# Mixer output normalized into its PSUM bank and added to the residual by VectorE for three batches, in place of GpSimd's sum of two SBUF buffers

## The reference

```python
x = x + layernorm(mixer(layernorm(x)))
x = x + layernorm(ffn(layernorm(x)))

def mixer(h):                       # Wi, Wf, Wg, Wo: 512 x 512
    i, f, g = h @ Wi.T, h @ Wf.T, h @ Wg.T
    gate = sigmoid(f)
    v = silu(i) * (1 - gate)
    o = scan over tokens of  s = gate * s + v
    o = rms_norm(o) * gnorm_w * silu(g)
    return o @ Wo.T
def ffn(h):                         # W1, W3: 2048 x 512, W2: 512 x 2048
    return fwht(silu(h @ W1.T) * (h @ W3.T)) @ W2.T
```

## Time and profile before

| what | value |
|---|---|
| median of 3 runs | 689.96 us |
| the profiled execution's own time | 689.71 us |
| its span, first to last instruction | 687.9 us |
| PE busy | 656.9 us, 95% |
| VectorE busy | 409.8 us, 60% |
| ScalarE busy | 352.8 us, 51% |
| GpSimd busy | 234.1 us, 34% |
| mean granted TensorE clock | 0.995 |

### The profile page before, as it was taken

The page is one execution under the profiler, slowest core; times in us unless marked ns, Lnnn a source line. Parts: engine busy times, 40 slices in busy tenths (PEclk is TensorE's granted clock), DMA queues, the critical chain, the costliest instruction groups (busy, mean ns, idle before and its releaser), DMA issues.

```text
span 687.9 us, 11542 instructions
## 1 busy us (share of the span) xinstructions
PE 656.9 (95%) x4339; PEld 427.8 (62%) x4340; DVE 409.8 (60%) x791; ACT 352.8 (51%) x629; POOL 234.1 (34%) x216
## 2 busy tenths in 40 slices
PE   3898999999999999999979999999999999999995
PEld 2444444444466677677757677777777777777672
DVE  5989898999999999884557113152222215322134
ACT  4999876473675756554525333353333334333332
POOL 1337366665751344164315111221121113121112
PEclk9999999999999999999999999999999999999999
DMA  8992543107344495993984332496223435435002
GB/s 318 406 404 103 129 117 62 61 7 179 122 160 132 169 280 146 329 300 113 266 274 174 111 108 108 136 299 224 108 108 126 170 134 192 146 120 200 3 1 91
DMA packets 60743, 114.12 MB, mean 166 GB/s; under 512 B 40464, under 2 KB 40720, under 8 KB 56080
## 3 DMA queue, kind: packets, MB, share of 16 engines
q1 hardware_dynamic: 60688, 113.39, 49.9%
HBM read 80.87 MB, written 23.07 MB: 151 GB/s over the span
## 4 chain that ended last, share of the span: by engine, by line
PE 64%; DVE 16%; ACT 7%; issue 5%; DVEq 3%; DMA 2%; POOL 2%; SPq 0%; POOLq 0%; ACTq 0%
PE ps L635 21%; PE ps L636 21%; PE ps L637 21%; DVEq L1052 3%; DVE st L1051 2%; ACT junk L914 1%; DVE o_s L1142 1%; ACT ring L835 1%; DMA out<-res 1%; DVE w2t L1306 1%; DVE w2t L1311 1%; DVE mv L1053 1%; ACT junk L921 1%; POOL w2t L1406 1%; DVE ring L1251 1%
## 5 line engine op out<-in xcount | busy, mean ns | idle before, releaser
L635 PE MATMUL ps<-xb,ring 128*128 128x256 f16 (+1 forms) x704 | 212.6, 302 | 3.5 <-DVE ring L1094 1.6
L637 PE MATMUL ps<-xb,ring 128*128 128x256 f16 (+1 forms) x704 | 212.6, 302 | 0.0
L636 PE MATMUL ps<-xb,ring 128*128 128x256 f16 (+1 forms) x704 | 212.6, 302 | 0.0
L1421 POOL TENSOR_TENSOR ring<-sga,ring 128x512 f16<-128x512 f32 x64 | 78.5, 1232 | 316.9 <-ACT ring L1007 316.9
L635 PE MATMUL ps<-ring 128*128 128x256 f16 x384 | 105.2, 274 | 4.4 <-DVE ring L1281 4.3
L636 PE MATMUL ps<-ring 128*128 128x256 f16 x384 | 105.0, 274 | 0.0
L637 PE MATMUL ps<-ring 128*128 128x256 f16 x384 | 105.0, 273 | 0.0
L635 PE MATMUL ps<-w2t,ring 128*128 128x512 f16 x256 | 97.0, 379 | 3.2 <-POOL ring L1421 3.2
L637 PE MATMUL ps<-w2t,ring 128*128 128x512 f16 x256 | 97.0, 379 | 0.0
L636 PE MATMUL ps<-w2t,ring 128*128 128x512 f16 x256 | 97.0, 379 | 0.0
L635 PEld LDWEIGHTS ps<-xb,ring 128*128 128x128 f16 x704 | 69.1, 98 | 40.8 <-issue 3.7
(11 more groups left out here) (165 smaller groups left out, 1033.4 us busy)
## 6 DMA issues: line engine op xcount, KB each, us to landing
ring<-w_comb SPq DMA_DIRECT2D x24, 1792.0 KB, 7.4
ring<-W13t SPq DMA_DIRECT2D x14, 1024.0 KB, 10.6
w_comb<-ring SPq DMA_DIRECT2D x8, 1792.0 KB, 7.0
rows<-L_attn_hidden_states SPq DMA_DIRECT2D x16, 256.0 KB, 5.3
w2t<-W2t SPq DMA_DIRECT2D x8, 512.0 KB, 13.6
res<-L_attn_hidden_states SPq DMA_DIRECT2D x16, 256.0 KB, 4.9
x_rows<-res SPq DMA_DIRECT2D x16, 256.0 KB, 3.4
x1r<-x_rows SPq DMA_DIRECT2D x16, 256.0 KB, 3.6
```

The costliest lines, as they stand in the source:

```text
L635: pe.matmul(dst, a_hi, b_hi, start=start, stop=False, skip_group_check=onto)
L636: pe.matmul(dst, a_hi, b_lo, start=False, stop=False, skip_group_check=onto)
L637: return pe.matmul(dst, a_lo, b_hi, start=False, stop=stop, skip_group_check=onto)
L1421: pool.tensor_tensor(hid(b, c, 1), sga[:, c % 2], hid(b, c, 0), ALU.subtract).then_inc(hid_lo, 1)
```

## The change

ScalarE writes the normed Y back into Y's own PSUM bank for mixer batches 0, 1 and 2, and VectorE adds that bank to `res[:, t]`, in a new step YA. The twelve GpSimd sums YN.0.t to YN.2.t go; batch 3 keeps the old way. The bank is now free only when VectorE's sum is done (`x1_rdy`). ScalarE's wait for the previous batch's sum (which protected the SBUF slot) goes, and GpSimd's YN.3.t gets a wait for the sums before it.

All five lists are written anew around this. Apart from YA and YN each engine runs the same steps as before, in another order; the banks are dealt anew too.

```diff
@@ wait_for_bank
             elif k == "Y":
-                engine.wait_ge(y_norm, TC * n + u + 1)
+                engine.wait_ge(x1_rdy if n < B - 1 else y_norm, TC * n + u + 1)
@@ ScalarE
             def yn(b, t):
                 act.wait_ge(y_ab, TC * b + t + 1)
-                if b > 0:
-                    act.wait_ge(x1_rdy, TC * (b - 1) + t + 1)
-                act.activation(y_rows(t), bank("Y", b, t)[:], ACT.Identity, bias=ab[:, 0, t:t + 1],
+                to = bank("Y", b, t)[:] if b < B - 1 else y_rows(t)
+                act.activation(to, bank("Y", b, t)[:], ACT.Identity, bias=ab[:, 0, t:t + 1],
                                scale=ysc[:, t:t + 1]).then_inc(y_norm, 1)
@@ VectorE
+            def add_residual(b, t):
+                dve.wait_ge(y_norm, TC * b + t + 1)
+                dve.wait_ge(ld_res[t], 16 * (b + 1))
+                dve.tensor_tensor(res[:, t], bank("Y", b, t)[:], res[:, t], ALU.add).then_inc(x1_rdy, 1)
@@ GpSimd
             def yn(b, t):
                 pool.wait_ge(y_norm, TC * b + t + 1)
+                pool.wait_ge(x1_rdy, TC * b + t)
                 pool.wait_ge(ld_res[t], 16 * (b + 1))
```

The parts of the lists that the prediction speaks of, old line first:

```diff
@@ PE_ORDER, start
-XT.0.3:3 AN.0.0:4 AN.1.0:5 GC.0.0:6 F.0.0:7 F.0.1:0 AN.2.0:1 AN.3.0:2 XT.1.0:3 XT.1.1:4
+XT.0.3:3 AN.0.0:4 AN.1.0:5 GC.0.0:6 AN.2.0:7 F.0.0:0 F.0.1:1 AN.3.0:2 XT.1.0:4 XT.1.1:3
@@ PE_ORDER, FFN batch 1, behind the last D of batch 0
-D.0.60 D.0.61 D.0.62 D.0.63 GQ.1.2 GU.1.1 GP.1.3 GR.1.2 GQ.1.3 GU.1.2 D.1.0 GP.1.4 D.1.1 D.1.2 GR.1.3
-D.1.3 D.1.4 D.1.5 D.1.6 GQ.1.4 D.1.7 GP.1.5 GU.1.3 GR.1.4 GU.1.4 GQ.1.5
+D.0.60 D.0.61 D.0.62 GP.1.3 D.0.63 GR.1.2 D.1.0 GU.1.2 GP.1.4 D.1.1 GQ.1.3 GQ.1.4 GR.1.3 GR.1.4 D.1.2
+GP.1.5 D.1.3 GU.1.3 D.1.4 D.1.5 GU.1.4 D.1.6 D.1.7 GP.1.6 GQ.1.5
@@ PE_ORDER, end
-GQ.3.14 GP.3.15 GR.3.14 GQ.3.15 D.3.48 GU.3.14 GR.3.15 D.3.52 GU.3.15 D.3.56 D.3.60 D.3.49
+D.3.36 D.3.37 GR.3.15 D.3.38 D.3.39 GU.3.15 D.3.40 ... D.3.47 D.3.48 D.3.52 D.3.56 D.3.60 D.3.49
@@ ACT_ORDER, ScalarE
-WN.2.0 AT.3.3 WQ.0.0 XT.1.2 ... G.0.2 S.0.1 P.0.1 I.0.3 WN.4.0 XT.1.3 G.0.3
+WQ.0.0 AT.3.2 XT.1.2 AT.3.3 ... G.0.2 F.0.3 S.0.1 P.0.1 WN.4.0 I.0.3 G.0.3 XT.1.3
@@ DVE_ORDER, FFN batch 1
-GU.1.1 UP.1.0 V.0.0 V.0.1 V.0.2 UP.1.1 V.0.3 GR.1.2 W.0.0 W.0.1 GU.1.2 GR.1.3 GU.1.3 W.0.2 W.0.3
-UP.1.2 Z1.3.0 Z1.3.1 Z2.3.0 Z2.3.1 Z1.3.2 UP.1.3 GR.1.4 Z1.3.3 GU.1.4
+GU.1.1 UP.1.0 UP.1.1 V.0.0 V.0.1 W.0.0 V.0.2 GR.1.2 GU.1.2 W.0.1 V.0.3 W.0.2 W.0.3 GR.1.3 GU.1.3
+UP.1.2 GR.1.4 GU.1.4 Z1.3.0 Z1.3.1 Z2.3.0 Z1.3.2 UP.1.3 Z2.3.1 Z2.3.2 Z1.3.3
@@ POOL_ORDER, GpSimd
-FW.0.5 X1.2.0 P.0.0 FW.0.6 FW.0.7
+FW.0.5 FW.0.6 P.0.0 FW.0.7 X1.2.0
@@ SP_ORDER
-NL.0.0 NL.1.0 NL.2.0 UL.0.0 NL.3.0 NL.4.0 UL.1.0 RL.0.0 ...
+UL.0.0 UL.1.0 UL.2.0 UL.3.0 NL.0.0 NL.1.0 UL.4.0 NL.2.0 UL.5.0 NL.3.0 UL.6.0 NL.4.0 UL.7.0 RL.0.0 ...
-WL.1.2 WL.1.3 O.0.0 LR.0.2 LR.0.3 O.0.1 LZ.3.0
+WL.1.2 ZD.2.4 ZD.2.5 ZD.2.6 WL.1.3 LR.0.2 O.0.0 LR.0.3 O.0.1 LZ.3.0
```

255 lines of the change are left out of this document (127 added, 128 removed).

## The result

The changed kernel is slower: 695.62 us (median of 4 runs, 694.72 to 697.37) against 689.74 for the kernel before on the same chip, a ratio of 1.0086 [1.0063, 1.0109], or 5.9 us more where I forecast 6.1 less. The four runs of the kernel before that this rests on (688.73 to 690.3) are on its quick side: beside the experiments it had medians of 691.0 to 692.5 us, and against those the changed kernel would be 3.1 to 4.6 us slower. The sign is sure, the 5.9 may be up to 3 us too much. The profiled execution took 697.37 us, 7.66 more than that of before; it is the slowest of the four runs, so what follows is read from a difference larger than that of the medians.

What follows compares the result with a forecast made beforehand. PE, busy 656.9 of 687.9 us, was taken as the bound, leaving its 31.0 us of standing still: 689.7 - 3.2 - 4.9 - 0.5 + 1.5 + 1.0 = 683.6, with 0.25 for the median 683.9 us; range 679.5 to 689.0.

Steps and rivals of the forecast that it cites:

- FFN batch 1: PE's stall at GU.1.4 and its slow clock, 5.65 us, go by doing VectorE's two sums before the norm: -4.9 us.
- the small stall: In FFN batch 1, a small PE stall in the passage up to GP.1.5: 0.7 us given back from 5.65.
- the stall moves: Rival: x1r as late as before, W.0.2 holds GR.1.3, PE waits at GP.1.5 with slow clock: 688.2 us, chance 0.17.
- The load: VectorE's twelve new sums between 77 and 190 us, 8.3 us less idle time and relief: +1.5 us charged.
- Y's bank, freed one VectorE operation later: PE steps behind YA, such as I.1.1, have another step before them, so the later release costs 0.
- The relief: Removing GpSimd's twelve sums stops them slowing VectorE: 3 us taken, between 0 and 11.4.
- The rival that VectorE starves PE: VectorE's 8.3 us paid in full from batch 1 on, two stalls with half clock: 692.5 us, chance 0.13.
- The start: Reordered first steps and W2's units loaded first: -0.5 us in all, bounds -1.5 and +1.5.
- The 1.2 us wait: At the start, PE's wait for GpSimd's butterfly L1406 ends but mostly moves to F.1.0, behind ScalarE's XT.1.3.
- the tail: End of PE's list: ten D steps, 6.5 us, cover the 3.23 us wait at D.3.56: -3.2 us.
- the tighter product order: PE's GU directly behind GR, and GP close behind GR, more often: 0.1 us for each of nine, +1.0 us.
- my two signs for being wrong: New PE waits over 3 us together between 190 and 330 us, or one of 3 us or more at GP.1.5 or GU.1.3.

Runs made afterwards that it cites:

- e2: Changed kernel's new lists with the old sum of two SBUF buffers put back on GpSimd: 692.91 us, ratio 1.0010 to the kernel before.
- e5: Changed kernel with VectorE's UP.1.3 moved ahead of Z1.3.0: 695.08 us, ratio 1.0048 to the kernel before.
- e4: Kernel before with GR.1.4, GU.1.4 and UP.1.3 ahead of Z1.3.0 in VectorE's list alone: 694.96 us, ratio 1.0033.
- e12: Kernel before with VectorE's new sum for batch 0 alone, GpSimd keeping the other sums: 694.87 us, ratio 1.0048.
- e7: Kernel before plus twelve VectorE operations that nobody waits for and that hold no bank, GpSimd's sums kept: 703.45 us, ratio 1.0166.
- e1: Kernel before, its lists kept, with VectorE's new sum in place of GpSimd's for batches 0 to 2: 700.20 us, ratio 1.0113.
- e10: Changed kernel with UP.1.3 ahead of Z1.3.0 on VectorE and GpSimd, and ScalarE's XT.1.3 ahead of WN.4.0: 695.71 us, ratio 1.0054 to the kernel before.
- e14: e10 and e6 together, with VectorE's XT.1.3 moved earlier and six more FFN batch 1 steps ahead of ZT.3 steps: 694.55 us, ratio 1.0039 to the kernel before.
- e3: Kernel before with six D steps moved behind GU.3.15 in PE's list alone: 686.51 us, ratio 0.9924.
- e15: e14 with the residual sum on GpSimd as in the kernel before: 693.45 us, ratio 1.0017 to the kernel before.
- e16: Kernel before with GpSimd's sums of batches 0 to 2 cut from 512 columns to 1, nothing in their place: 690.71 us, ratio 0.9977.
- e11: e7 with GpSimd's sums of batches 0 to 2 cut from 512 columns to 1: 699.32 us, ratio 1.0101 to the kernel before.
- e18: Changed kernel with the next batch's norm spread in three engines' lists through FFN batch 1, and e6's SyncE order: 690.79 us, ratio 0.9993 to the kernel before.
- e6: Changed kernel with SyncE's transposes ZD.2.4 to ZD.2.6 ahead of the weights' load WL.1.2: 693.11 us, ratio 1.0027 to the kernel before.

## Why the prediction was wrong

It failed in the sign, by 12 us (5.9 more for 6.1 less), at three terms of its sum and at a passage for which it had none. The lists' shares below are from the account, one execution each.

*FFN batch 1, taken as -4.9.* The lists alone gave -0.45 (e2's 5.71 against 6.16), and with the sums the passage is 1.7 us worse. The first half of the step was good: the reload went out 3.5 us behind D.0.60 (3.6 forecast) and was 8.3 us on its way (6.7), W.0.3 let go at 359.9 us, and PE waited 0.8 us before GP.1.5, the small stall for which I gave back 0.7. The failed sentence is "the next user of Z1.3, GU.1.5, stands further down". I followed VectorE's list only as far as the two sums. UP.1.3, behind Z1.3.2, gates ScalarE's UP.1.3, and the seed GP.1.5 stands behind that. e5 shows it: with UP.1.3 ahead of the norm the 3.73 us before GQ.1.5 go (and others come). The recorded rival "the stall moves" had the direction but another place, GP.1.5 behind W.0.2. e4 shows the same thing in the kernel before: the two sums moved ahead cost 2.3 us where I had expected -4.9 of that idea.

*The load, taken as +1.5.* It is +5.2 under the new lists and +7.8 under the old ones. In the account of the changed kernel against e2, 3.1 us of it lie at 180 to 245 us and 2.2 in FFN batch 1. That batch 0's four sums cost nothing held under the new lists, though the idle time alone doesn't do it (e12: +3.3 under the old ones). That Y's bank, freed one VectorE operation later, costs 0 was nearly right: PE waits 1.5 us for the new sum in all, at two places behind 184 us. What failed is the netting of length against idle time and relief in batches 1 and 2 (8.3 - 2.8 - 1.4 - 3). The idle time in the earlier trace rows was no room for them: e7's operations, which nobody waits for, cost at least about what they last. The relief was right in kind (3 taken; VectorE is busy for 2.7 to 4.4 us less without GpSimd's sums), but in the time it is 4.1 with a wide interval where VectorE is overloaded and 1.6 where it isn't. The rival that VectorE starves PE had this mechanism and, at 692.5, the side; it too took the -4.9 in FFN batch 1 as earned. The Trainium skill ("Perfetto Trace Analysis", section "Optimizing Scalar/DVE Operations"), which suggests taking work from a saturated VectorE, agrees with e1 and e7, which give it work and lose 7.8 and 11.5 us. The other page of the Trainium skill that I used ("SBUF — State Buffer", section "Who interferes with whom") agrees as well: the new sum, with one SBUF input, lasted 665 to 691 ns all twelve times.

*The passage from 180 to 245 us.* I forecast nothing for it from the lists. They cost 3.8 us there by themselves (e2's 5.78 against 1.96) and the sums 3.1 more. PE waits 2.0 us before GQ.0.1 (0.8 in e2) and 1.9 before GR.0.2 (1.9 in e2). Before GQ.0.1 ScalarE's list holds the seed (L959) behind 5 us of other work and a wait of 0.5 us for VectorE:

```profile
203.52 2.19 ACT L949 ACTIVATE ring<-ring,w_s 128x1024 f16<-128x1024 f32 x2 [0.53 <-DVE ring L1266]
...
207.10 0.57 ACT L959 ACTIVATE ps<-ps 128x512 f32<-128x512 f32 x1
```

*The start, taken as -0.5.* It is +0.6 in e2 (2.2 before G.1.0 less 1.6 before F.1.2). The 1.2 us wait did move to F.1.0, as I said, but as 2.8 us (0.85 before) with a half clock, and the late half of XT.1.3 is VectorE's (e10 against e14), not ScalarE's.

*Right:* the tail (3.2 taken; 3.4 in the account, and e3 proves it alone); the tighter product order, as far as two quiet passages tell (+1.0 taken; those before D.1.2 and before GU.3.15 come to +0.2); the length of the sum, VectorE's busy time, GpSimd's nearly. Of my two signs for being wrong the first came, over 3 us of new waits between 190 and 330 us (6.8 us of waits from 184 to 250 us, against 1.0 before). The second did not as written: GP.1.5 and GU.1.3 waited 0.8 us and nothing, and the 3.73 us stood nine steps behind GP.1.5, at GQ.1.5.

The parts, from the forecast to the result: 4.4 us for the lists in batch 1, 3.8 for the lists at 180 to 245 us, 1.1 for the start, 3.7 for the sums, less 0.8 for the product order and 0.2 for the tail. That makes 12.0. The match is closer than its parts are known: each of the two ratios behind the 5.2 us is good to some 1.5 us, and the account of before and after differs by more than their medians.

What stays open: which steps of the new lists make the 3.8 us at 180 to 245 us (none was undone there by itself), and how much of the sums' cost would remain with lists made for them; e14 and e15 leave 1.1 to 1.5 us, with an interval that is wider.

## What to carry to other kernels

With an order written by hand for each engine, follow a late input through every list: an operation that is not needed can hold a needed one on a second engine and a third. If a repair moves a stall instead of ending it, look for the lump of work behind it and spread that in all the lists. Before giving a nearly full engine more work, put in operations of that length which nobody waits for: here they cost 11.5 us (9.1 to 13.8) for 9.7 us of their own, and told in one run what an argument about idle shares had missed.

## What the runs showed of the hardware

The same wait costs different amounts. At the end of the kernel before PE stands 3.23 us; in the profiled execution of the earlier trace rows the clock stayed at 1.00 after it, but in e16, with the same wait of 3.23 us, it fell:

```profile
672.00:673.00 1.00, 1.00 (x3) 0.29 (x2) 0.00 (x0) 0.00 (x0) 0.00 (x0) 0.50 0.00 0
...
676.00:677.00 1.00, 1.00 (x4) 0.41 (x3) 0.64 (x1) 0.27 (x1) 0.00 (x0) 0.50 0.00 0
```

It stayed there from 671 to 677 us, and the passage cost 6.17 us instead of 3.38. Seven of the kept traces have this wait of 3.23 us. In two (before, e12) the clock stayed at 1.00 and the last passage cost 3.38 us; in five (e1, e4, e7, e11, e16) it fell, and the passage cost 4.7 to 6.2. Their mean is 4.6 us, which would explain most of what e3 gains by having no such wait (5.3 us, 3.5 to 7.0). The spread of the runs agrees: the kernel before lay between 688.8 and 694.9 us in those on one chip, e3 between 686.1 and 687.7. Likewise the changed kernel's 2.84 us before F.1.0 brought 0.50 for the next 3 us, and the passage cost 3.8 us in all, while e18's 2.33 us in the same place left the clock at 1.00. So the stalls of 2.8 to 3.7 us in these kernels weren't priced by their length alone: the clock could add as much again.

SyncE's row for a transpose was 6.77 us behind the issue of a 1.8 MB load and 1.34 us ahead of it. The reload of `x1r` was not delayed by this long row, since it had to wait for W.0.0 anyway (issued at 349.47 and 349.79 us); the next weights' load was, by some 4 us, and e6, which has the short row, was the faster kernel.
